# One variance, another bank and ends by stage in the expert phases; residual and normalisation of the second cross attention on ScalarE and Pool

## The reference

```python
_layernorm(x): (x - mean) / sqrt(var + 1e-5)
# layer 0
x = _layernorm(x + self_attention(x))           # 16 heads, window of 32
x = _layernorm(x + cross_attention(ctx, ctx, x))  # one head
x = _layernorm(x + experts0(x))     # 8 experts, 512 hidden, gelu, best 2 of 8
# layer 1
x = _layernorm(x + state(x))        # state(x) begins with a layernorm with gain and bias of its own
x = _layernorm(x + tanh(gate) * (attention16(ln(x), ctx) @ w_out + b_out))
x = _layernorm(x + experts1(x))     # 8 experts and a shared one, 256 hidden, silu
```

## Time and profile before

| | us |
|---|---|
| median of 3 runs (lowest to highest) | 1886.55 (1885.76 to 1887.1) |
| the profiled execution, its own time | 1884.88 |
| its span | 1883.0 |
| PE busy | 1667.1 (89%) |
| DVE busy | 1549.9 (82%) |
| ACT busy | 1275.3 (68%) |
| POOL busy | 925.5 (49%) |
| DMA queue 1, share of 16 engines | 64.2% |

### The profile page before, as it was taken

One profiled execution on the slowest core, in us unless ns is written; L12 is line 12 of the kernel. 1 busy time (PEld: TensorE's weight loads), 2 busy tenths in 40 slices (PEclk: granted clock), 3 DMA queues, 4 the chain that ended last, 5 costly groups with the idle time before them and its releaser, 6 DMA issues. The chain is left out here.

```text
span 1883.0 us, 34675 instructions
## 1 busy us (share of the span) xinstructions
PE 1667.1 (89%) x10425; PEld 1009.4 (54%) x10425; DVE 1549.9 (82%) x2885; ACT 1275.3 (68%) x2106; POOL 925.5 (49%) x723
## 2 busy tenths in 40 slices
PE   4987996889957899999999999999999999994997
PEld 2654665777733344554554554454455455454886
DVE  2765785877758999999999999999999999975887
ACT  2442332877735887887888788788788888864554
POOL 3640111363335766565665656656567465421333
PEclk9997998799978999999999999999999999997998
DMA  5203884311100898988899898898888889973231
GB/s 190 95 0 127 306 332 173 85 42 45 45 34 17 180 197 174 199 182 179 190 183 190 183 190 187 178 195 182 179 199 179 188 183 185 182 135 122 47 79 29
DMA packets 632266, 281.85 MB, mean 150 GB/s; under 512 B 601852, under 2 KB 606236, under 8 KB 631452
## 3 DMA queue, kind: packets, MB, share of 16 engines
q1 hardware_dynamic: 632204, 281.10, 64.2%
HBM read 129.02 MB, written 1.05 MB: 69 GB/s over the span
## 5 line engine op out<-in xcount | busy, mean ns | idle before, releaser
L2237 DVE SCALAR_TENSOR_TENSOR xa_h<-xa_psum,xa_rinv,xa_h 128x500 f16<-128x500 f32 x672 | 452.8, 730 | 1.0 <-ACT xa_h L2445 0.7
L2445 ACT ACTIVATE xa_h<-xa_psum,xa_rinv 128x1000 f16<-128x1000 f32 x448 | 371.5, 883 | 51.8 <-DVE xa_rinv L2228 51.5
L2429 ACT ACTIVATE xa_psum<-xa_psum,xa_bias,unscale_s 128x1500 f32<-128x1500 f32 x224 | 353.2, 1577 | 7.4
L2073 PE MATMUL xa_psum<-xa_c_hi,xa_q_hi 128*128 128x500 f16 x672 | 257.4, 383 | 54.5 <-DVE xa_h L2237 50.1
L2217 DVE TENSOR_REDUCE xa_psum<-xa_psum 128x1 f32<-128x1000 f32 x224 | 269.3, 1202 | 14.2 <-PE xa_psum L2075 13.4
L2098 PE MATMUL xa_psum<-xa_prT,xa_n_hi 128*128 128x512 f16 (+1 forms) x768 | 270.8, 353 | 3.6 <-issue 1.6
L2100 PE MATMUL xa_psum<-xa_prT,xa_n_lo 128*128 128x512 f16 (+1 forms) x768 | 270.6, 352 | 0.0
L2099 PE MATMUL xa_psum<-xa_prT,xa_n_hi 128*128 128x512 f16 (+1 forms) x768 | 270.6, 352 | 0.0
L2074 PE MATMUL xa_psum<-xa_c_lo,xa_q_hi 128*128 128x500 f16 x672 | 252.7, 376 | 0.0
L2075 PE MATMUL xa_psum<-xa_c_hi,xa_q_lo 128*128 128x500 f16 x672 | 252.4, 376 | 0.0
L1939 POOL TENSOR_SCALAR xa_ctxT<-xa_ctxT,scales 128x1500 f32<-128x1500 f32 x31 | 126.3, 4073 | 166.4 <-DMA xa_ctxT<-in_ctxT 166.4
(11 more groups left out here) (328 smaller groups left out, 3630.4 us busy)
## 6 DMA issues: line engine op xcount, KB each, us to landing
ctxN<-in_ctxP SPq DMA_DIRECT2D x16, 1536.0 KB, 9.5
xa_ctxP<-in_ctxP SPq DMA_DIRECT2D x32, 768.0 KB, 4.3
ctxT<-in_ctxT SPq DMA_DIRECT2D x16, 1500.0 KB, 6.4
xa_ctxT<-in_ctxT SPq DMA_DIRECT2D x32, 750.0 KB, 4.7
moe_spread<-weight_rows SPq DMA_DIRECT2D x16, 1024.0 KB, 8.4
xa_prT<-xa_h SPq DMA_TRANSPOSE x192, 5.5
up<-in_F_up SPq DMA_DIRECT2D x1, 2048.0 KB, 7.7
down<-in_F_down SPq DMA_DIRECT2D x1, 2048.0 KB, 11.8
```

The source lines that it names most:

```text
L2073: nc.tensor.matmul(out, qh, c_hi[:, b, a:z], start=True, stop=False)
L2237: nc.vector.scalar_tensor_tensor(low, psum[:, bank + a:bank + z, 0:W], rinv[:, s % 2, :], high, ALU.mult, ALU.subtract).then_inc(h2_ready, 1)
L2429: nc.scalar.activation(psum[:, bank:bank + 3, 0:W], psum[:, bank:bank + 3, 0:W], ACT.Exp, bias=bias[:, s % 2, :], scale=k.unscale_s[:, :], ...
L2445: nc.scalar.activation(h[:, H_SLOT[s], 0, a * W:z * W].rearrange("p (a c) -> p a c", c=W), psum[:, bank + a:bank + z, 0:W], ACT.Identity, ...
```

## The change

In the expert phases:

- The inner normalisation of layer 0 no longer takes statistics of the normalised rows. If v is the variance of r, the variance of the normalised rows is v / (v + eps), so the two normalisations together are (r - mean) times the power -1/2 of v (1 + eps) + eps². Pool computes this root from the first variance, VectorE makes both results from r, the inner one first, the outer one a place later.
- The features are turned for pair e-2 instead of e-3, into bank 6 + e % 2, where the residual's product is. TensorE waits there until VectorE has read the residual of pair e-1; `project` no longer waits for the store.
- The last chunk's tail is a `drain`: every stage is done for all four pairs before the next, with a bank per pair; Pool's roots and its copy are one instruction for four pairs.

In the second cross attention:

- ScalarE sums the gated bias rows (`sum_x`, step 7), multiplies the output product by the gate and sums it (`gate`, step 9), and sums the squares of r - mean (`square`, step 11), each an activation with `accum_out`.
- Pool adds the residual, computes the negated mean, the variance, the root and the normalised rows (`residual`, `normalise`), behind the same split as before. `gated` moves ahead of the scaling for the next pair.
- VectorE's residual, statistics and normalisation go. TensorE's turn in step 10 waits for `yg_ready` (ScalarE) instead of `r_ready`.

```diff
-            for e in range(1, CK + 3):
-                for at in range(-1, 3):
-                    tail(CHUNKS - 1, e, at, after=True)
+            drain(CHUNKS - 1)
...
+            def inner_root(i, p):                                   # Pool
+                pool.wait_ge(t.mean_var_ready, n(i, p))
+                pool.tensor_scalar(t.var_eps2[:, p, :], t.mean_var[:, p, 1:2], 1.0 + EPS, EPS * EPS, ALU.mult, ALU.add)
...
+                pool.tensor_tensor(t.rstd2[:, p, :], t.var_eps2[:, p, :], k.minus_half[:, :], ALU.pow)
...
                 def project(e):                                     # TensorE
                     pe.wait_ge(part_ready, slot(i, e))
-                    if not first and not final and 0 <= e - 3:
-                        pe.wait_ge(t.feat_stored, last(i, min(e - 2, CK), CK))
...
-                    pe.wait_ge(part_ready, this(i + 1, e - 1, NE))
-                    t.tensor_transpose(pe, i, e - 3, psum[:, 4 + e % 2, 128:256])
+                if at == 2 and 0 <= e - 2 < CK and not final:
+                    pe.wait_ge(t.r_ready, this(i, min(e, CK), CK))
+                    if e >= 4:
+                        pe.wait_ge(t.feat_stored, this(i, e - 3, CK))
+                    t.tensor_transpose(pe, i, e - 2, psum[:, 6 + e % 2, 128:256])
...
+            def drain(i):                                           # VectorE; the others likewise
+                for p in range(CK): ...  r = psum[:, p, 0:128] + x_tok
+                for p in range(CK): ...  bn_stats
+                for p in range(CK): ...  bn_aggr
+                if inner: ...            xn2 of four pairs, after Pool's rstd2
+                for p in range(CK):
                     t.vector_normalise(dve, i, p)
-                    if inner:
-                        t.vector_inner_moments(dve, i, p)
...
+            def residual(i):                                        # Pool, second cross attention
+                pool.wait_ge(yg_ready, this(i))
+                pool.tensor_tensor(t.r[:, :, :], yg[:, :, :], xg[:, :, :], ALU.add)
+                pool.tensor_scalar(neg_mean[:, :], y_sum[:, :], x_sum[:, :], -1.0 / D, ALU.add, ALU.mult)
+            def normalise(i):
+                pool.wait_ge(squares_ready, this(i))
+                pool.tensor_scalar(t.var_eps[:, 0, :], squares[:, :], 1.0 / D, k.eps[:, :], ALU.mult, ALU.add)
+                pool.tensor_tensor(t.rstd[:, 0, :], t.var_eps[:, 0, :], k.minus_half[:, :], ALU.pow)
+                pool.tensor_scalar(t.xn[:, 0, :], t.r[:, 0, :], neg_mean[:, :], t.rstd[:, 0, :], ALU.add, ALU.mult)
+                t.pool_store(pool, i, 0)
...
                 split_n(i, 0, first)
+                if not first:
+                    gated(i - 1)
...
                 split_n(i, 1)
                 if not first:
-                    gated(i - 1)
-                    t.pool_rstd(pool, i - 1, 0)
-                    t.pool_store(pool, i - 1, 0)
+                    residual(i - 1)
+                    normalise(i - 1)
...
                 if u == TURNED[0] and r == 1 and not first:
-                    pe.wait_ge(t.r_ready, this(i - 1))
+                    pe.wait_ge(yg_ready, this(i - 1))
...
-                if s == RESIDUAL and not first:                     # VectorE
-                    residual(i - 1)
...
-                    if s == NORMALISE:
-                        t.vector_normalise(dve, i - 1, 0)
...
+            def sum_x(i):                                           # ScalarE
+                nc.scalar.activation(yg[:, 0, :], xg[:, 0, :], ACT.Identity, accum_out=x_sum[:, :])
+            def gate(i):
+                nc.scalar.activation(yg[:, 0, :], psum[:, 7, 0:128], ACT.Identity, scale=k.gate_tanh[:, :],
+                                     accum_out=y_sum[:, :]).then_inc(yg_ready, 1)
+            def square(i):
+                nc.scalar.activation(yg[:, 0, :], t.r[:, 0, :], ACT.Square, bias=neg_mean[:, :],
+                                     accum_out=squares[:, :]).then_inc(squares_ready, 1)
...
                 exponentials(i, s)
+                if s == min(OUTPUT) and not first:
+                    sum_x(i - 1)
+                if s == max(OUTPUT) and not first:
+                    gate(i - 1)
+                if s == SQUARES and not first:
+                    square(i - 1)
```

More of the change, by code:

```diff
@@ L1248, in expert_phase, with run @@
         out_stored, hi_ready, lo_ready = sem("out_stored"), sem("hi_ready"), sem("lo_ready")
+        rooting = sem("rooting")
         block = ctx.enter_context(nc.Block())
-        def run(engine, chunk, tail):
+        def run(engine, chunk, tail, drain):
             chunk(0, lambda e, at: None, first=True)
@@ L1311, in chunk, with tail @@
                         .then_inc(acc_ready, 1)
-            def tail(i, e, at, after=False):
+            def tail(i, e, at):
                 if at != 1:
@@ L1425, in tail, with drain @@
                     pe.wait_ge(t.r_ready, this(i, e - 2, CK) if e >= 3 else last(i, CK, CK))
+                    if not final:
+                        pe.wait_ge(t.feat_stored, this(i, e - 3, CK) if e >= 4 else last(i, CK, CK))
                     nc.tensor.transpose(psum[:, 6 + e % 2, 0:128], mixed[:, 2 * (e - 1):2 * e, :], k.ident[:, :])\
                         .then_inc(y_ready, 1)
[L1428 to L1438 removed]
+                if at == 2 and 0 <= e - 2 < CK and not final:
[3 more added lines that the diff above has]
+                    t.tensor_transpose(pe, i, e - 2, psum[:, 6 + e % 2, 128:256])
+            def drain(i):
+                pe.wait_ge(acc_ready, this(i, NE - 1, NE - 1))
+                pe.wait_ge(t.r_ready, last(i, CK, CK))
+                for p in range(CK):
+                    nc.tensor.transpose(psum[:, p, 0:128], mixed[:, 2 * p:2 * p + 2, :], k.ident[:, :]).then_inc(y_ready, 1)
+                if not final:
+                    for p in range(CK):
+                        t.tensor_transpose(pe, i, p, psum[:, p, 128:256])
+            run(pe, chunk, tail, drain)
         @block.vector
@@ L1563, in tail @@
                     t.vector_moments(dve, i, p)
+                if inner and at == 1 and 0 <= e - 2 < CK:
+                    t.vector_normalise(dve, i, e - 2)
                 if at != -1:
@@ L1629, in chunk, with tail, drain @@
                         x_high(i + 1)
-            def tail(i, e, at, after=False):
-                if at == 2 and 0 <= e - 3 < CK and not final:
-                    t.scalar_store(act, i, e - 3, psum[:, 4 + e % 2, 128:256])
-            run(act, chunk, tail)
+            def tail(i, e, at):
+                if at == 2 and 0 <= e - 2 < CK and not final:
+                    t.scalar_store(act, i, e - 2, psum[:, 6 + e % 2, 128:256])
+            def drain(i):
+                if not final:
+                    for p in range(CK):
+                        t.scalar_store(act, i, p, psum[:, p, 128:256])
+            run(act, chunk, tail, drain)
 def expert_phase0(k):
@@ L2515, in epilogue @@
                         evacuate(*at)
+                sum_x(PAIRS - 1)
+                gate(PAIRS - 1)
+                square(PAIRS - 1)
                 t.scalar_store(act, PAIRS - 1, 0, psum[:, 7, 128:256])
```

131 lines of the change are left out of this document (102 added, 29 removed).

## The result

The kernel after takes 1866.0 us (median of 4 runs, 1862.0 to 1867.7) beside 1886.4 us (1885.8 to 1887.1) for the kernel before on the same chip: a ratio of 0.9898, 95% interval 0.9886 to 0.9910, so 19 us faster, 17 to 21.5. The forecast was 1868.0 with a range of 1860 to 1878. The profiled execution's span fell from 1883.0 to 1864.3 us. Cut at the same instructions in both traces, the 18.7 us come out as follows; a stretch ends with the start of the named instruction, unless the end of one is meant. The table leaves out the last pair's output products, which take the same time in both, and the state stage and the routing of layer 1, which together take 0.2 us more.

What follows compares the result with a forecast made beforehand. Most second cross attention steps follow a ring of VectorE and ScalarE, with TensorE nearly equal to VectorE in step 10. Terms -8.5 + 1.0 - 1.0 - 6.3 - 3.5 = -18.3 us from 1886.55 give 1868.25, rounded to 1868.0; range 1860 to 1878.

Steps and rivals of the forecast that it cites:

- Second cross attention, VectorE: Step 10 of each pair: removing 1.06 us of VectorE work brings 0.57 before TensorE binds, 15 times, -8.5 us.
- ScalarE at nothing: Second cross attention: three added activations per pair, about 0.36 us each, fit into ScalarE's waits; price 0.
- the rival of 1893 us: Second cross attention: Square changes the activation table, two loads per pair, +25 us, 1893 us in all; chance 0.06.
- Pool just in time: Second cross attention: Pool's normalised rows end at 1202.9, before TensorE asks for them at 1203.17.
- TensorE waiting for Pool's normalisation: Second cross attention: a listed sign that the forecast is wrong; no size given.
- The term of 0: Second cross attention: Pool's added work per pair was to cost nothing in the looped pairs, 0 us.
- the second half of the argument: Second cross attention: up to 0.85 us of lateness of Pool's rows falls in TensorE's pause.
- End of the stage: Last pair of the second cross attention, without cover: from 2.29 to 3.3 us, +1.0 us (0.5 to 1.6).
- Experts of layer 0: First expert phase, chunks 1 to 3: stalls removed against new waits, about -1 us; bounds +6 and -10.
- The ring: First expert phase, experts 2 to 4: ScalarE, low part, residual, feature transpose, ScalarE's next start; 6.6 us per round.
- End of layer 0: Four pairs' tail in the first expert phase, run stage by stage: -6.3 us (-5 to -7).
- of layer 1: Four pairs' tail in the second expert phase, run stage by stage: -3.5 us (-3 to -4.2).

Runs made afterwards that it cites:

- `light_before`: Kernel before with four of the five output products of step 9 left out, so the output differs: 0.9985 of the kernel before, -2.8 us.
- `light_after`: Kernel after with four of the five output products of step 9 left out, so the output differs: 0.9856 of the kernel before.
- `exp_only`: Kernel before with only the expert phases of the change, second cross attention as before: 0.9925 of the kernel before, -14.1 us.
- `pair_end`: Kernel after with both expert phases' ends one pair behind the other, still one variance: 0.9945 of the kernel before, +8.8 us against the kernel after.
- `act_double`: Kernel after with each pair's square done twice on ScalarE: 0.9900 of the kernel before, +0.4 us against the kernel after.
- `pool_late`: Kernel after with three unused 128x128 additions on Pool behind its wait for the squares: 0.9934 of the kernel before, +6.8 us against the kernel after.
- `res_early`: Kernel after with the first expert phase's residual ahead of each expert's fourth low part: 0.9854 of the kernel before, -8.3 us against the kernel after.
- `res_mid`: Kernel after with the first expert phase's residual ahead of each expert's third low part: 0.9833 of the kernel before, -12.3 us against the kernel after.

## Why the prediction was right

- **Second cross attention, VectorE** (forecast -8.5, measured -8.1). The step that mattered, to read the saving against TensorE, held: `light_before` and `light_after` show that 0.49 us of the 1.06 is TensorE's. The pair takes 66.97 us, the forecast's 66.96. That this agrees to 0.01 is in part luck: without any edit to the stage the looped pair moves by up to 0.1 us from kernel to kernel (67.45 in `exp_only` against 67.52 before, 66.87 in `pair_end` against 66.97 after).
- **ScalarE at nothing**: right; `act_double` shows it even with 0.39 us more. I priced the activation at 0.36 with the read of the accumulator, at most 0.5; the three take 0.30 to 0.39 alone, 0.39 to 0.49 with the read. **No table load** came with the square: the rival of 1893 us is excluded by the groups by line of ScalarE in the second cross attention, where this is the only load:

```profile
L2547 ACT ACT_TABLE_LOAD x1 | 1.3, 1283 | 0.0
```

  The Trainium skill (ScalarE: Activation LUTs, "Table sets: the hidden batching unit") does not name Square among the functions of every set; here it needed no load between two Exps, 15 times.
- **Pool just in time**: not quite. The normalisation takes 0.45 (taken: 0.5, bounds 0.45 to 1.1), but from the exponential's sum to the end of the rows it is 2.57 us (1254.82 to 1257.39), not the 2.3 of the forecast. The hand-overs are the reason: 0.30 us from the squares to Pool and 0.41 before the normalisation, where the forecast has 0.3 for all waits beyond the 0.93. So the rows come 0.18 us behind TensorE's turn instead of ahead of it, and "TensorE waiting for Pool's normalisation", which the forecast named as a sign of being wrong, is there in every pair. The term of 0 stands, because the second half of the argument held: the lateness falls in TensorE's pause, and `pool_late` shows that a further 1.28 us costs only 0.28 per pair.
- **End of the stage** (+1.0, bounds 0.5 to 1.6, measured +1.9): outside its bounds. The instructions were priced well, 3.1 us against 2.9; the hand-overs were not. The forecast leaves 0.2 us for them, and they take 1.25 of the chain's 4.19: the chain crosses between ScalarE and Pool three times, at 0.09 to 0.31 us, and waits 0.18 and 0.40 between Pool instructions, the longer one where several waits stand in front.
- **Experts of layer 0** (-1.0, measured -2.6): the largest miss, though within its bounds. The ring was found with its length: 6.6 us forecast, 6.55 measured, and `res_early` and `res_mid` show its cause. A slip in the sum is part of the miss: two chunks at -0.85 and one at -0.1 are -1.8, not -1.0. The rest is that the gains behind the ring were priced too small: expert 5 went from 6.14 to 4.99 (forecast -0.9), the last expert with its change of chunk from 8.43 to 7.35 (-0.8), and in the last chunk the last expert's start to the first residual from 10.2 to 9.0. Against it, expert 2 lost 1.7 us instead of 1.4.
- **End of layer 0** (-6.3, bounds -5 to -7, measured -7.7) and **of layer 1** (-3.5, measured -4.0): the mechanism as forecast, the order by stage shown by `pair_end`. The size was off, in layer 0 beyond its bounds, mostly because I took the small instructions' price from the state stage: 0.53 and 0.65 us there, 0.2 here. They ran beside VectorE's work there and not here; that this is the reason was not tried.
- The sum was closer than its terms, and that is luck: it missed by +0.9 at the stage's end, +0.4 in the pairs and +1.7 ahead of the change, which is no effect of it, against -1.6, -1.4 and -0.5 in the expert phases.

## What to carry to other kernels

A saving on the engine that seems to bound a step is worth only the distance to the next engine in that step; read that distance before, and afterwards ask for the cheapest work to move off the engine that is now late. A wait put in to share a bank can close a ring through another engine's program order; moving the reader forward in its own queue opened it here at no cost (-12.3 us in `res_mid`). At a phase's end, where nothing covers a chain, run the pairs stage by stage and keep the shortest chain even if the loop uses another. A view that shows no wait of TensorE doesn't prove that there is none: compare the distance of two starts with that in a kernel where nothing is late.

## What the runs showed of the hardware

- Pool did three additions of 128x128, each waiting for the one before, in 1.35 us, 0.45 each; its one column power took 0.57 and one of four columns 1.02. A small instruction on one or four columns took 0.19 to 0.27 in the stage's loop and at the phases' ends, and 0.19 to 1.63 in the state stage.
- TensorE took Pool's rows 0.14 to 0.15 us after they ended, whether the view shows a wait or not.
- A normalisation of 128x128 with two operands per partition took 0.45 us on Pool and 0.35 on VectorE.
- ScalarE's sum over 128 elements is a second instruction of 0.19 us that overlaps the first by 0.1.
- TensorE's 128x500 products took 0.62 us, 0.42 apart, at the granted clock of 0.50 and 0.37, 0.21 apart, at 1.00. A step that met the low stretch with its scores lost 1.2 us; from 720 to 1600 us the granted clock is 1.00.
